# Cross-attention and a spline-weight feed-forward: both sides of each residual cell from TensorE, chosen by a predicated copy

## The reference, cut to what matters

```python
# x (4, 512, 512), context (4, 512, 256)
def attention(x_norm, ctx):                    # einsum names shortened
    q = ctx @ Wq.T + bq;  k = ctx @ Wk.T + bk  # (512, 128)
    att = softmax(q @ k.T)                     # (512, 512)
    return x_norm @ att.T

def ffn(h):                                    # 2048 inner features
    gate_w, up_w = spline(gate_cp, 2048, 512), spline(up_cp, 2048, 512)
    down_w = spline(down_cp, 512, 2048)
    return (silu(h @ gate_w.T) * (h @ up_w.T)) @ down_w.T

x = x + attention(layernorm(x), ctx)
x = x + ffn(layernorm(x))
```

## Time and profile before

| | |
|---|---|
| Median of 3 launches | 291.2 us (287.96 to 291.93) |
| Span of the profiled execution | 286.6 us |
| TensorE matmul busy | 267.5 us, 93% |
| VectorE, ScalarE, GpSimd busy | 182.0, 125.3, 131.5 us |
| Chain that ended last | TensorE 73%, VectorE 12%, ScalarE 5%, DMA 2% |
| First feed-forward matmul starts | 71.14 us |

### The profile page before, as it was taken

How to read it: one execution, slowest core, us unless ns; L and a number is a source line. 1 busy time by engine, 2 the same in 40 slices (tenths; PEclk the granted TensorE clock), 3 DMA queues, 4 the chain that set the end, 5 groups by cost and what they waited for, 6 DMA issues and landing times.

```text
span 286.6 us, 3824 instructions
## 1 busy us (share of the span) xinstructions
PE 267.5 (93%) x1250; PEld 169.7 (59%) x1252; DVE 182.0 (64%) x322; ACT 125.3 (44%) x202; POOL 131.5 (46%) x138
## 2 busy tenths in 40 slices
PE   7698579999999999999999999999999999599995
PEld 3232167654655768956548588655385887264674
DVE  0799977887558665744568737646587477363403
ACT  3036633335667703157677222557674133354300
POOL 0587362579654712218618123078083131594800
PEclk9959959999999999999999999999999999999999
DMA  7998053000710000034400000325000001100003
GB/s 193 338 432 363 7 155 141 0 2 0 301 67 0 3 0 2 0 146 165 201 0 0 0 0 0 138 80 222 0 0 0 0 0 73 73 0 2 0 0 146
DMA packets 7210, 23.29 MB, mean 81 GB/s; under 512 B 1185, under 2 KB 2337, under 8 KB 5793
## 3 DMA queue, kind: packets, MB, share of 16 engines
q1 hardware_dynamic: 7200, 23.18, 21.6%
HBM read 18.98 MB, written 4.19 MB: 81 GB/s over the span
## 4 chain that ended last, share of the span: by engine, by line
PE 73%; DVE 12%; ACT 5%; issue 4%; DMA 2%; POOL 1%; SPq 1%; ACTq 0%; DVEq 0%; POOLq 0%
PE bank L1298 11%; PE bank L1344 10%; PE bank L1300 9%; PE bank L1318 6%; PE bank L1150 5%; PE bank L1247 4%; PE bank L1249 4%; PE bank L1248 4%; PE bank L1161 4%; PE bank L1351 3%; DVE prod L849 3%; PE bank L1204 3%; DMA power<-in_g_power 2%; PE bank L1274 2%; DVE inter L940 1%
## 5 line engine op out<-in xcount | busy, mean ns | idle before, releaser
L1100 POOL TENSOR_TENSOR ih<-inter,ones 128x512 fp32r<-128x512 f32 x64 | 65.7, 1042 | 37.8 <-DVE inter L940 36.3
L940 DVE TENSOR_TENSOR inter<-inter,bank 128x512 f32<-128x512 f32 x64 | 43.4, 686 | 26.1 <-ACT inter L755 26.0
L755 ACT ACTIVATE inter<-bank 128x512 f32<-128x512 f32 x64 | 37.7, 599 | 25.1 <-PE bank L1300 24.5
L1344 PEld LDWEIGHTS bank<-d_r,ih 128*128 128x128 f32 x256 | 30.6, 192 | 4.2 <-issue 3.2
L726 ACT ACTIVATE qk<-bank,nmr,rstd 128x512 f32<-128x512 f32 x16 | 12.5, 780 | 46.8 <-PE bank L1249 46.8
L1298 PE MATMUL bank<-xh,gate_r 128*128 128x512 f32 x64 | 29.9, 468 | 1.5 <-DVE zg L932 1.5
L1344 PE MATMUL bank<-d_r,ih 128*128 128x192 f32 x256 | 31.1, 274 | 0.0
L1318 PE MATMUL bank<-inter,d_u 128*64 128x512 f32 x128 | 30.1, 602 | 0.0
L1298 PE MATMUL bank<-xh,up_r 128*128 128x512 f32 x64 | 27.2, 425 | 1.4 <-DVE inter L940 1.3
L1084 POOL TENSOR_TENSOR xres<-x,ones 128x2048 f32<-128x2048 f32 x4 | 14.4, 3602 | 23.9 <-DMA out<-xres 23.6
L1300 PE MATMUL bank<-zg,gate_v 102*128 102x512 f32 x64 | 25.3, 396 | 0.0
(11 more groups left out here) (100 smaller groups left out, 461.7 us busy)
## 6 DMA issues: line engine op xcount, KB each, us to landing
x<-in_x SPq DMA_DIRECT2D x4, 1024.0 KB, 4.7
xT<-in_xT SPq DMA_DIRECT2D x4, 1024.0 KB, 6.8
out<-xres SPq DMA_DIRECT2D x16, 256.0 KB, 2.1
ctxT<-in_ctxT SPq DMA_DIRECT2D x4, 512.0 KB, 7.6
rd<-in_d_r SPq DMA_DIRECT2D x2, 768.0 KB, 7.3
knots<-in_d_knot SPq DMA_DIRECT2D x1, 1280.0 KB, 12.3
d_coef<-in_d_coef SPq DMA_DIRECT2D x1, 1024.0 KB, 16.9
d_pt<-in_d_node SPq DMA_DIRECT2D x1, 1024.0 KB, 18.3
```

What stands on the lines that cost most here:

```text
L755: nc.scalar.activation(inter[:, m], gbank[m % 2][:], ACT.Silu).then_inc(s["silu_done"], 1)
L940: V.tensor_tensor(inter[:, m], inter[:, m], ubank[m % 2][:], ALU.mult).then_inc(s["mult_done"], 1)
L1100: G.tensor_tensor(ih[:, m], inter[:, m], ones[:, 0].broadcast_to([P, TOK]), ALU.mult).then_inc(s["ih_done"], 1)
L1344: mm(in_blocks(obank[t][:], i // CLS), ih[:, m, t * P:(t + 1) * P], d_r[:, i], start=m == 0, stop=False, skip_group_check=True)
```

## The change

- A residual piece is now made as two whole candidates. TensorE makes the cell's polynomial as it holds left of the break and as it holds right of it, in fp32 from 32 rows, into two banks. A byte mask (`g_after`, `d_after`) says which weights lie right of the break, and VectorE copies the right candidate over the left one there (`copy_predicated`, PSUM to PSUM). ScalarE rounds the bank into `gate_r`, `up_r` or `d_r`. GpSimd has no part in it. `spread` now handles two pieces at a time.
- For the down side GpSimd multiplies a table by the jumps and adds (`tables`); the bf16 splits go (`split_windows`, the last part of `jumps`).
- `powers` moves to VectorE; `split_x` of the first batch moves to GpSimd; `down_nodes` is cut into `down_taps` and the rest.
- The order of loads and of the preamble is new: the attention's loads and `qk` come first, 16 of the 20 `keep_warm` go.
- `project` writes four products of 32 columns to four quarters of the bank.
- The wait for `dv_done` moves from before `zg`, `gate_up` and `xres` to the ninth `activate` and to `down_tail`.

Two new functions on the host: `gate_cell` and `down_cells` give the polynomials.

```diff
-def cell_residual(pos, left, right, knot):
+def gate_cell(pos, left, right, first, mid, half):
+    shift = np.polynomial.Polynomial([mid, half])
+    value, slope = (h((pos - left) / (right - left)) for h in (lambda u: hermite(u)[2], lambda u: hermite(u)[3]))
+    x, e, width = shift + (pos * STEP - first), shift + (right * STEP - first), (right - left) * STEP
+    before = [-(value * e**2 + slope * width * 2 * e), -(value * e**3 + slope * width * 3 * e**2)]
+    return before, [before[0] + x**2, before[1] + x**3]
+def down_cells(left, right, knot):
...
+    width = (right - left) * STEP
+    e, x = (right - knot) * STEP, (knot - left) * STEP
+    sides = []
+    for value, slope in ((e**2, 2 * e * width), (e**3, 3 * e**2 * width)):
+        sides.append([slope - 3 * value, 2 * value - slope])
+    for value, slope in ((x**2, -2 * x * width), (-x**3, 3 * x**2 * width)):
+        sides.append([3 * value + slope, -slope - 2 * value])
+    return np.where(inside, np.array(sides).reshape(2, 2, 2, *knot.shape), 0), inside
...
+            m = 2 * DOWN_ORDER[r - 2 * CLS]
+            return m, m + 1
+        def weights(r):
+            if r < 2 * CLS:
+                return gu_r[r // CLS][:, r % CLS]
+            m = tile_pair(r)[0]
+            return d_r[:, m:m + 2].rearrange("p m n -> p (m n)")
+        def is_after(r):
+            if r < 2 * CLS:
+                return g_after[:, r % CLS]
+            m = tile_pair(r)[0]
+            return d_after[:, m:m + 2].rearrange("p m n -> p (m n)")
         def attention_only(st):
```

TensorE:

```diff
-                    if r >= 2:
-                        pe.wait_ge(s["res_mul"], 2 * (r - 1))
                     if r in (0, CLS):
-                        pe.wait_ge(s["win_split"], r // CLS + 1)
+                        pe.wait_ge(s["power_done"], r // CLS + 1)
                     if r == 0:
-                        pe.wait_ge(s["pick_in"], 16)
+                        pe.wait_ge(s["cell_in"], 16)
                     if r == 2 * CLS:
-                        pe.wait_ge(s["jump_split"], 2)
-                    for k in range(2):
-                        dst = bank[2 * (r % 2) + k]
-                        if r < 2 * CLS:
-                            c = slice(r % CLS * WROWS, (r % CLS + 1) * WROWS)
-                            last = mm(dst[:], pick[c, k], win_hl[c, r // CLS], start=True, stop=True)
-                        else:
-                            for n in range(2):
-                                m = 2 * (r - 2 * CLS) + n
-                                for part, row in pieces(dst[:, n * STRIP:(n + 1) * STRIP], jump[k], m // CLS):
-                                    last = mm(part, spread_[:, m], row, start=True, stop=True)
-                    last.then_inc(s["res_mm"], 1)
+                        pe.wait_ge(s["table_done"], 1)
+                        pe.wait_ge(s["shape_in"], 16)
+                    for side in range(SIDES):
+                        for q in (r, r + 1):
+                            if side == 0 and q >= 2:
+                                pe.wait_ge(s["res_done"], q - 1)
+                            dst = bank[2 * (q % 2) + side]
+                            if q < 2 * CLS:
+                                c = slice(q % CLS * WROWS, (q % CLS + 1) * WROWS)
+                                last = mm(dst[:], g_cell[c, side], weighted[c, q // CLS], start=True, stop=True)
+                            else:
+                                for n, m in enumerate(tile_pair(q)):
+                                    w = m // CLS
+                                    c = slice(QUAD * w, QUAD * (w + 1))
+                                    last = mm(like_blocks(dst[:, n * STRIP:(n + 1) * STRIP], w), d_shape[c, side, m % CLS],
+                                              in_blocks(d_table[c, 0, side], w), start=True, stop=True)
+                            if side == 1:
+                                last.then_inc(s["cell_mm"], 1)
                 def prob_t(b, t):
...
                     for a in range(CLS):
-                        half = slice(a % 2 * HALF, (a % 2 + 1) * HALF)
-                        last = mm(zgbank[half], g_basis[:, a], xn2T[:, a], start=a < 2, stop=a >= 2, skip_group_check=True)
+                        last = mm(zgbank[a * QUAD:(a + 1) * QUAD], g_basis[:, a], xn2T[:, a], start=True, stop=True, skip_group_check=True)
                     last.then_inc(s["zp_mm"], 1)
...
                         pe.wait_ge(s["zd_done"], b + 1)
+                        pe.wait_ge(s["dv_done"], 1)
                     for z, v in ((0, 0), (0, 1), (1, 0)):
```

VectorE and ScalarE:

```diff
                 def residual(r):
-                    dve.wait_ge(s["res_mm"], r + 1)
                     if r == 0:
-                        dve.wait_ge(s["r_in"], 32)
-                    if r >= 2:
-                        dve.wait_ge(s["res_done"], r - 1)
+                        dve.wait_ge(s["after_in"], 16)
                     if r == 2 * CLS:
-                        dve.wait_ge(s["rd_in"], 32)
-                    n = r % CLS if r < 2 * CLS else r - 2 * CLS
-                    for k, part in enumerate((r2g, r3g) if r < 2 * CLS else (rd2, rd3)):
-                        width = HID if r < 2 * CLS else 2 * STRIP
-                        V.tensor_tensor(prod2[:, r % 2, k, 0:width], bank[2 * (r % 2) + k][:, 0:width], part[:, n * width:(n + 1) * width], ALU.mult).then_inc(s["res_mul"], 1)
+                        dve.wait_ge(s["dafter_in"], 16)
+                    dve.wait_ge(s["cell_mm"], r + 1)
+                    after = is_after(r)
+                    left, right = (bank[2 * (r % 2) + side][:, 0:after.shape[1]] for side in range(SIDES))
+                    V.copy_predicated(left, after, right).then_inc(s["picked"], 1)
                 def prob_t(b, t):
                     pass
...
                 def residual(r):
-                    pass
+                    act.wait_ge(s["picked"], r + 1)
+                    if r == 2 * CLS:
+                        act.wait_ge(s["node_mm"], 2 * CLS)
+                    dst = weights(r)
+                    nc.scalar.activation(dst, bank[2 * (r % 2)][:, 0:dst.shape[1]], ACT.Copy).then_inc(s["res_done"], 1)
...
                     act.wait_ge(s["g_mm"], MT * b + m + 1)
+                    if m == MT // 2:
+                        act.wait_ge(s["dv_done"], 1)
                     nc.scalar.activation(inter[:, m], gbank[m % 2][:], ACT.Silu).then_inc(s["silu_done"], 1)
...
                     dve.wait_ge(s["jump_c"], 1)
-                    dve.wait_ge(s["jump_d"], 1)
-                    V.scalar_tensor_tensor(jb, knots[:, 0], S2 / S3, knots[:, 2], ALU.mult, ALU.add).then_inc(s["jump_d"], 1)
-                    for k in range(2):
-                        dve.wait_ge(s["jump_hi"], k + 1)
-                        V.tensor_tensor(jump[k][HALF:P], (ja, jb)[k][HALF:P], jump[k][HALF:P], ALU.subtract).then_inc(s["jump_split"], 1)
+                    dve.wait_ge(s["jump_done"], 1)
+                    V.scalar_tensor_tensor(jump[:, 1], knots[:, 2], 6.0, knots[:, 0], ALU.mult, ALU.add).then_inc(s["jump_done"], 1)
+                def tables():
```

GpSimd:

```diff
+                    if first(b):
+                        pool.wait_ge(s["consts_set"], 1)
+                        pool.wait_ge(s["xt_in"], 16)
+                        G.tensor_tensor(xh[:], xT[:], ones[:].broadcast_to([P, NT, TOK]), ALU.mult).then_inc(s["xh_done"], 1)
+                        pool.wait_ge(s["xh_done"], 1)
+                        G.tensor_tensor(xl[:], xT[:], xh[:].bitcast(f32), ALU.subtract).then_inc(s["xsplit_done"], 1)
...
+                def tables():
+                    pool.wait_ge(s["table_in"], 16)
+                    for k in range(2):
+                        pool.wait_ge(s["jump_done"], k + 1)
+                        G.tensor_tensor(d_table[:, k], d_table[:, k], jump[:, k:k + 1].broadcast_to([P, SIDES, HID]), ALU.mult).then_inc(s["table_mul"], 1)
+                    pool.wait_ge(s["table_mul"], 2)
+                    G.tensor_tensor(d_table[:, 0], d_table[:, 0], d_table[:, 1], ALU.add).then_inc(s["table_done"], 1)
```

More of the change, by code:

```diff
@@ L303, in xattn_spline_ffn_kernel @@
         zg = sb("zg", [G_K, TOK], f32r)
-        ja, jb = (win[:, n] for n in range(2))
-        jump = [knots[:, 3 + n, 0:HID // 2].bitcast(bf16) for n in range(2)]
         def in_blocks(row, w):
@@ L367, in attention_only @@
-            st.residual(2)
-            st.keep_warm(7)
-            st.residual(3)
-            for t in range(8, 10):
-                st.keep_warm(t)
-            st.spread(2)
-            st.powers(1)
-            st.node_weights(0)
-            st.spread(3)
+            for t in range(2):
+                st.energy(0, t)
+                st.softmax(0, t)
+            for u in range(2):
+                st.node_weights(u)
+            for t in range(2, 4):
+                st.energy(0, t)
+                st.softmax(0, t)
@@ new lines, in attention_only @@
+            st.powers(1)
+            for u in range(2, 4):
```

(83 more changed lines are left out.)

307 lines of the change are left out of this document (122 added, 185 removed).

## The result

| | before | after |
|---|---|---|
| Median of the launches on the same chip | 290.86 us (4, 287.96 to 291.93) | 301.66 us (4, 300.51 to 303.19) |
| Ratio, 95% interval | | 1.038 (1.033 to 1.044) |
| Profiled execution: span, mean granted clock | 286.6 us, 0.976 | 300.2 us, 0.932 (its own time 302.34) |
| First gate matmul of the four passes | 71.14, 130.27, ..., 248.22 | 86.31, 144.46, 202.60, 260.63 |
| Preamble; last pass | 71.1; 38.4 us | 86.3; 39.6 us |

The change makes the kernel 3.8% slower; the forecast was 290.2 us. The four starts say where: the preamble is 15.2 us longer, each of the first three passes about 1.0 shorter (58.1 for 59.1), the last 1.2 longer. 15.2 - 2.8 + 1.2 = 13.6, the difference of the spans.

The account below looks back on a forecast made before the run. TensorE's work was taken to bound the passes, waits the preamble's end. Span 286.6 + 1.6 (preamble with clock falls) - 2.6 (`project`) = 285.6; on the median 291.2 - 1.0 = 290.2 us, range 284.5 to 296.

Parts of the forecast that it names:

- The preamble, followed down the new order: Preamble chain summed step by step at full clock: ends at 68.9 us, 2.2 shorter than before.
- the last scaling ends at 22.2: Preamble, VectorE and ScalarE alternating on picks, maxima, exponentials and node corrections: last scaling done at 22.2 us.
- `jumps` 1.9: Preamble, VectorE after `stats` and two corrections: `jumps` takes 1.9 us, before picks 4-5 ending at 37.3.
- `split_x` 3.6 + 4.9 ends at 24.1, hidden: Preamble, GpSimd after xT lands near 15.5: split done at 24.1 us, hidden since `pl` ends at 28.5.
- I take +3.8 in all: Preamble: TensorE clock falls in the new holes cost 3.8 us, so it ends at 72.7, 1.6 later than before.
- The tail: Preamble from `xm(3)` ending at 51.8 to 69.2 at full clock; a clock fall from 57 to 67 adds 3.1 us.
- The slower rival: Preamble: clock falls in the hole at 18.6, stays low before the first pass; 298.3 us, chance 0.05.
- `project`: Once a pass on TensorE: four quarters share the array, 0.86 us less each, 2.6 us over three passes.
- The copy: VectorE's predicated copy in the residual: taken as 0.60 us, between 0.41 and 1.2; dear-copy rival 294 to 296 us, chance 0.1.
- The table load: ScalarE, end of preamble: 1.28 us, before hidden under `project`, now stands behind the last copy; zp at 65.7.
- or if GpSimd's `tables` end after 44: Sign that the forecast is wrong; preamble `tables` on GpSimd were expected from 34.9 to 42.3 us.
- Full clock and no hold-ups: Preamble sum without clock falls: 69.2 us, 68.9 corrected; the rival with full clock gives 286.4 us, chance 0.2.

Follow-up runs that it names:

- Experiment 5: Changed kernel plus a measurement behind its last output, VectorE instructions beside a GpSimd one; launched once for its trace; four scalings, among others, took 4.2 to 4.3 us more.
- experiment 1: Changed kernel with second weighting, GpSimd's knot sums and `tables` moved apart from VectorE's SBUF-only work: 293.44 us, ratio 1.019 to the kernel before, gate 77.85.
- experiment 6: Changed kernel with the first batch's `split_x` back on ScalarE and VectorE, behind `scale`: 299.88 us, ratio 1.039 to the kernel before, gate 84.10.
- Experiment 2: Changed kernel with 73 products on ones in TensorE's preamble holes, nothing moved: 296.03 us, ratio 1.029 to the kernel before, gate 79.68, mean clock 0.994.
- experiment 7: Changed kernel with twelve filler products in the last pass alone, behind `project` and `replicate`: 300.70 us, ratio 1.039 to the kernel before; last pass 38.3 us.
- experiment 4: Kernel before with only `project` changed, four products on four quarters of the bank: 285.94 us, ratio 0.990 to the kernel before, gate 70.67.
- experiment 10: Changed kernel reordered, `split_x` off GpSimd, fillers added, `tables` behind `mean_shift`, `down_nodes` last and on VectorE: 286.85 us, ratio 0.987 to the kernel before, gate 71.90.

## Why the prediction was wrong

**The step that failed** is "The preamble, followed down the new order", in the prices it gave VectorE: "the last scaling ends at 22.2", "`jumps` 1.9", and "`split_x` 3.6 + 4.9 ends at 24.1, hidden". GpSimd did end in time, at 22.27, earlier than forecast; what it did to VectorE meanwhile was not priced. The durations were taken from rows where GpSimd stood still, or of kinds that it doesn't hold (a PSUM operand, statistics): the scaling of 1.67 us at 35.32 has an idle GpSimd beside it in the stretch from 34 to 36. Experiment 5 shows the mechanism, experiment 1 its worth: 8.5 us, the clock that a hold-up pulled down included. On the chain the hold-ups are 2.7 (the up side's product is held 4.1, but without it VectorE would wait for ScalarE: in experiment 6 the scaling starts at 21.61, not 24.26), 2.7 (scaling) and 2.0 (`jumps`) = 7.4.

**The clock: the mechanism right, the term too small.** "I take +3.8 in all". Experiment 2 shows some 5.9 with the hold-ups. The tail went as worked out: 66.0 to 86.3 is 20.3 us, against 17.4 + 3.1. The front is the difference. `xm(1)` took 5.4 us in place of 2.73, `spread(6)` 4.37 in place of 1.7, and the first transposes 1.94 and 1.71 in place of about 1.06, behind holes that the hold-ups had lengthened: 9.00 in place of 3.6, and 4.08 ahead of `spread(6)`. The slower rival came nearest in time, 298.3, and was still too low; its clock, low without a break from 22 to 70, is not what happened (22.5 to 32.5, 43 to 56.5, 70 to 84).

**The clock in the last pass** was not in the sum: 1.2 us, shown in experiment 7.

**`project` was right**: 1.06 us for 8 records, 0.88 less, 2.6 in three passes (experiment 4). The price of the Trainium skill (TensorE: Matmul & The Clock Gate, packing small matmuls), by which I had estimated 1.9, is too careful here, and its rule that weight loads overlap products in flight only in another row strip isn't borne out: the quarters share the strip, and their 8 records take 1.06.

**The copy was right**: 1.29 us for two predicated copies of 128x512, 1.02 of 128x384, so 0.60 and about 0.48 from one to the next, and never held by GpSimd. xT landed at 13.6 (forecast 15.5). The table load lay open, as forecast, 80.66 to 81.94. The condition "or if GpSimd's `tables` end after 44" came true, at 50.4, but by the lateness handed on to it.

**Full clock and no hold-ups** is the case the sum was written for, 69.2 for the gate matmul; experiment 10 is nearest to it and reads 71.90. So the sum is some 2.7 us too low even there. The last scaling ends 1.2 late (23.41 for 22.2), `spread(6)` starts 2.3 late (39.76 for 37.5), `xm(3)` ends 3.7 late (55.5 for 51.8), and 1.0 comes back in the tail, although experiment 10's own placing of `down_nodes` costs 0.5 there. One term is plain: a down pair was put at 1.3 us and takes 1.6 (63.32 to 64.93). What else makes up the rest is open.

**Two readings** were off and changed nothing: the clock's line in the earlier trace rows has two low slices and not four, and four fp32 records of 0.43 with a tail of 0.17 make 1.89 us, not the 1.98 of the row.

## What to carry to other kernels

When work moves to GpSimd, "hidden" has two sides. Lay its new instructions on VectorE's timeline and mark those of VectorE's that have both inputs in SBUF, or copy or scale from SBUF: each such pair can cost up to the whole of the other's instruction, however small the held one is. Put GpSimd's long instructions beside those of VectorE that have a PSUM operand, and look again after each move, because the next pair slides in; which pair meets can depend on when a load lands (experiment 2). And an idle stretch of TensorE is paid twice when the clock falls behind it, so mend the wait before adding fillers.

## What the runs showed of the hardware

- Four VectorE instructions behind a GpSimd instruction of 4.50 us take 4.2 us more than alone if they scale, round, or have two SBUF operands; a PSUM bank less an SBUF operand, a predicated copy in PSUM and statistics of an SBUF tile take nothing more. In the other direction a 1.27 us sum of GpSimd's took 3.18.
- Four fp32 products on four column quarters run at once: 8 records in 1.06 us, against 1.94 on two halves, over the same rows of weights.
- A predicated copy of 128x512 from PSUM to PSUM by a byte mask takes 0.68 us, the same as a product of a PSUM bank with an SBUF operand.
- At the same two holes of 1.5 us the clock fell in the last pass of seven profiled kernels and not in that of an eighth.
